# Copies of the transposed probabilities: heads innermost, half on ScalarE and half on VectorE

## The chip, the cores and the metric

One NeuronCore of a Trainium2 chip. The kernel is one launch; the metric is the device time in microseconds. Engines are named as in the profile: PE (TensorE) multiplies matrices, ACT (ScalarE) applies functions and copies, DVE (VectorE) does element-wise work and reductions, POOL (GpSimd) does element-wise work on SBUF, SP starts DMAs. PE writes into PSUM (eight banks, each 512 floats per partition here); ACT and DVE read it out.

## The reference

A small vision tower over 64 images: patches of 16 x 16 are embedded, with a class token that makes 37 tokens of 256 numbers per image. Then follow an attention with 16 heads of 16 and one shared key and value, a gated low-rank MLP, a recurrent attention, and an expert MLP with one of 8 experts per token. All is float32. The change lies in the first attention:

```python
q = (jnp.einsum('bte,oe->bto', x, Wq) + bq) * scaling
kv = jnp.einsum('bte,oe->bto', x, Wkv) + bkv
k, v = (kv[..., :HEAD_DIM], kv[..., HEAD_DIM:])
qr = q.reshape(bsz, NUM_HEADS * tgt_len, HEAD_DIM)
attn_weights = jnp.einsum('brd,bsd->brs', qr, k)
attn_probs = jax.nn.softmax(attn_weights, axis=-1)
attn_output = jnp.einsum('brs,bsd->brd', attn_probs, v)
attn_output = attn_output.reshape(bsz, NUM_HEADS, tgt_len, HEAD_DIM)
attn_output = attn_output.transpose(0, 2, 1, 3).reshape(bsz, tgt_len, EMBED_DIM)
out = jnp.einsum('bte,oe->bto', attn_output, Wo) + bo
```

The reshape of q is taken without a transpose, so the rows of an image are numbered token * 16 + head, and the output reads them in that order.

## The kernel before, in words

The kernel runs in phases with a barrier between them. The first, about the first 300 us, is embedding, attention and the logits of the gate. Images are padded to 66 and go in 22 tiles of three; two tiles are a group, so there are 11 groups, and each group has three pairs of images. The phase is a software pipeline written out by hand: a Python loop `for i in range(-1, PAIRS + 1)` on each engine issues one turn per step, in a fixed order, and the engines meet only by semaphores. In turn i PE works on the three pairs p = 3i, 3i+1, 3i+2 of group i, and puts beside them the embedding and the first transposes of group i+1 and the output projection and second transposes of group i-1. An engine takes its instructions strictly in order, so a waiting instruction holds back all that stands behind it.

What a pair of images goes through:
- `scores` (L383, PE): four products into banks 4 and 5, 16 heads x 37 keys, rows 0 to 36 for one image and 64 to 100 for the other.
- `shift_scores` (L538, L541, DVE): maximum per head, and subtraction, into the buffer `prob[p % 2]`.
- `exponentials` (L601, ACT), `sum_probs` (L549, L551, DVE), `scale_probs` (L692, POOL).
- `turn_probs` (L393, PE): eight transposes of 128 columns (two heads) each into banks 6 and 7. The even head of each two lands on partitions 0 to 36, the odd one on 64 to 100.
- `copy_probs` (L609, ACT), twice: out of PSUM into `pt`, first the even heads, then the odd ones. `pt` holds for each image 37 x 16 numbers per partition with the head innermost. Each copy walks the eight chunks outermost and the tokens innermost, so it reads PSUM contiguously and writes one float every 64 bytes.
- `mix_values` (L413, PE): 16 products of `pt` with the values, then `copy_output` (L620, ACT).

PE waits in `mix_values(p)` for both copies of p, in `turn_probs(p)` for both copies of p-1 and for `scale_probs(p)`. The copies of p wait for `mix_values(p-1)`. On PE a turn runs: scores(3i), embedding (L329), turn_probs(3i-1), embedding, mix_values(3i-1), scores(3i+1), turn_probs(3i), project(i-1) (L425), mix_values(3i), turn_first(i+1) (L340), scores(3i+2), turn_probs(3i+1), values and keys(i+1) (L371, L359), mix_values(3i+1), turn_second(i-1) (L436), queries(i+1) (L351), gate_logits(i-1) (L449). turn_first waits for `normalise_first` and turn_second for `normalise_second` (both L504, DVE); the next scores wait for `copy_queries` (L643, ACT). On POOL `spread_keys` (L683) stands between the scalings. The add of the projection on DVE is L558, its statistics L493 to L498.

Of the kernel before, what the change touches and what calls it, by code (L numbers as in the profile page):

```python
# [21 lines left out]
B, TOK, D = 64, 37, 256  # L22
# [7 lines left out]
HH = NH // 2  # L30
# [9 lines left out]
HP = 64  # L40
# [28 lines left out]
def build(nc, x_h, pack1_h, pack2_h, packc_h, w1_h, w2_h, out_h):  # L69
# [9 lines left out]
    with ExitStack() as top:  # L79
# [178 lines left out]
        with phase():  # L258
# [3 lines left out]
             v_out, k_block, scored, maxed, shifted, exped, row_sum, row_inv, scaled, p_turned, p_copied, mixed, o_copied,  # L262
# [5 lines left out]
                    "row_inv", "scaled", "p_turned", "p_copied", "mixed", "o_copied", "with_bo", "projected", "added",  # L268
# [29 lines left out]

            def probs_of(p):
                return prob[p % 2].rearrange("p (f h s) -> p f h s", f=2, h=HH)[:, :, :, 0:TOK]  # L300
# [13 lines left out]
            def _(pe):  # L314
# [72 lines left out]
                def turn_probs(p):  # L387
                    if not image_pair(p):
                        return
                    pe.wait_ge(scaled, p + 1)  # L390
                    free(pe, p_copied, 2 * p)
                    for c in range(HH):
                        mm = nc.tensor.transpose(turns_bank[:, c * 128:c * 128 + PR],  # L393
                                                 prob[p % 2][:, c * 128:(c + 1) * 128], ident[0:PR, 0:PR])
                    mm.then_inc(p_turned, 1)

                def mix_values(p):
# [4 lines left out]
                    pe.wait_ge(p_copied, 2 * (p + 1))  # L402
# [75 lines left out]
            def _(dve):  # L478
# [64 lines left out]

                def sum_probs(p):
# [27 lines left out]
                for i in range(-1, PAIRS + 1):  # L572
                    p = 3 * i
                    shift_scores(p)
                    sum_probs(p)
                    add_embedded(i + 1)
                    shift_scores(p + 1)
                    normalise_first(i + 1)
                    sum_probs(p + 1)
                    add_projected(i - 1)  # L580
                    shift_scores(p + 2)
                    normalise_second(i - 1)
# [5 lines left out]
            def _(act):  # L588
# [15 lines left out]
                def copy_probs(p, e):  # L604
                    if not image_pair(p):
# [3 lines left out]
                    nc.scalar.copy(  # L609
                        pt.rearrange("p (m t c e) -> p c m t e", m=2, t=TOK, e=2)[:, :, :, :, e],  # L610
                        turns_bank[e * HP:e * HP + TOK, :].rearrange("p (c m t) -> p c m t", c=HH, m=2)[:, :, :, 0:TOK]
                    ).then_inc(p_copied, 1)
# [33 lines left out]
                for i in range(-1, PAIRS + 1):  # L646
                    p = 3 * i
                    exponentials(p)
                    copy_probs(p - 1, 0)
                    copy_probs(p - 1, 1)  # L650
                    copy_output(p - 1)
                    copy_probs(p, 0)
                    exponentials(p + 1)
                    copy_probs(p, 1)
                    copy_output(p)
                    copy_first(i + 1)
                    copy_probs(p + 1, 0)
                    exponentials(p + 2)
                    copy_probs(p + 1, 1)
# [1241 lines left out]
```

## Time and profile before

| | us |
|---|---|
| median of 3 runs | 902.04 (899.74 to 902.21) |
| profiled execution | 892.15 |
| its span | 890.1 |
| PE busy in the span | 686.8 (77%) |
| DVE busy | 434.1 (49%) |
| ACT busy | 284.2 (32%) |
| L609, both copies of 33 pairs (66) | 76.5, 1159 ns each |

The profile comes from one execution. Its span runs from the first to the last instruction; 2.05 us of the execution's time lie around it. "Idle before" is the time for which an engine stood still ahead of an instruction, and the releaser is what the profile holds to have ended it. L609 and the like are lines of the kernel before; in the changed kernel the same instructions have other numbers. PEclk is the clock granted to PE as a share of 2.4 GHz.

### The profile page before, as it was taken

The numbers are of one execution on the slowest core, as the hardware profiler recorded it, in microseconds if no ns is written. First come the engines' busy times: TensorE is split into PE (matmuls) and PEld (weight loads), VectorE is DVE, ScalarE is ACT, GpSimd is POOL, SyncE is SP. The second block draws the span as 40 slices with busy tenths as digits, with TensorE's granted clock in tenths as the row PEclk, the third lists the DMA queues.
The fourth block names the chain that finished last, engine by engine and source line by source line (L and its number), as shares of the span: only waits on it lengthen the run. The fifth ranks groups of instructions, "written<-read, shape, count | busy, mean of one in ns | idle before, by whom it ended". The sixth has DMA issues, their size and how long they took to land. (4 is left out here: it accounts for less than half of the span.)

```text
span 890.1 us, 14154 instructions
## 1 busy us (share of the span) xinstructions
PE 686.8 (77%) x4606; PEld 521.2 (59%) x4606; DVE 434.1 (49%) x1183; ACT 284.2 (32%) x648; POOL 246.8 (28%) x330
## 2 busy tenths in 40 slices
PE   3789888888886418999996200399549999999995
PEld 2557666666663306888885100388445677666773
DVE  1355555555564282666766349366542333333331
ACT  0244454444454222434423100154302222222221
POOL 2334344344443000434343100134111222222211
PEclk9899999999999557999998555599758999999998
DMA  8111001011100000000000677332421111111110
GB/s 339 32 32 32 21 28 30 20 32 32 32 1 1 1 0 3 1 0 0 0 0 0 31 270 330 64 88 85 171 96 42 42 48 54 54 53 44 48 42 18
DMA packets 21542, 49.31 MB, mean 55 GB/s; under 512 B 12451, under 2 KB 12581, under 8 KB 20719
## 3 DMA queue, kind: packets, MB, share of 16 engines
q1 hardware_dynamic: 17583, 33.21, 12.8%
q0 software_dynamic: 3328, 10.23, 3.8%
q10 hardware_dynamic: 576, 5.15, 1.5%
q8 instruction: 33, 0.54, 0.3%
q14 instruction: 22, 0.18, 0.1%
HBM read 38.72 MB, written 9.86 MB: 55 GB/s over the span
## 5 line engine op out<-in xcount | busy, mean ns | idle before, releaser
L1793 ACT ACTIVATE work<-psum,cst 128x128 f32<-128x128 f32 x208 | 56.6, 382 | 144.1 <-PE psum L1708 144.1
L1695 PE MATMUL psum<-arena_w,work 128*128 x208 | 96.7, 609 | 1.0 <-DVE work L1747 1.0
L1719 PE MATMUL psum<-arena_w,work 128*128 x416 | 94.2, 379 | 0.4 <-ACT work L1793 0.4
L609 ACT COPY arena_w<-psum 37x592 f32<-37x592 f32 x66 | 76.5, 1159 | 54.4 <-PE psum L393 53.6
L1719 PEld LDWEIGHTS psum<-arena_w,work 128*128 128x128 f32 x416 | 77.1, 190 | 10.5 <-issue 1.1
L1352 PE MATMUL psum<-tokens,work 111*111 (+1 forms) x88 | 15.8, 305 | 73.0 <-POOL work L1320 71.8
L1756 DVE COPY work<-psum 128x512 f32<-128x512 f32 x52 | 36.0, 692 | 70.9 <-PE psum L1695 70.9
L1657 POOL DMA_INDIRECT out<-work,row_i x26 | 25.7, 987 | 161.0 <-DVE work L1769 161.0
L329 PE MATMUL psum<-arena_w 128*111 128x256 f32 x264 | 63.0, 390 | 8.7 <-DMA arena_w<-in_pack 8.7
L692 POOL TENSOR_TENSOR arena_w<-arena_w,work 101x592 f32<-101x592 f32 x33 | 39.5, 1197 | 91.5 <-DVE work L551 91.5
L1695 PEld LDWEIGHTS psum<-arena_w,work 128*128 128x128 f32 x208 | 38.6, 196 | 40.4 <-issue 40.4
L329 PEld LDWEIGHTS psum<-arena_w 128*111 128x111 f32 x264 | 45.9, 180 | 22.9 <-DMA arena_w<-in_pack 8.7
L250 POOL TENSOR_TENSOR work<-work 111x1 f32<-111x1 f32 x44 | 24.4, 555 | 118.8 <-DVE work L246 118.8
L1352 PEld LDWEIGHTS psum<-tokens,work 111*111 111x111 f32 x88 | 11.7, 188 | 74.1 <-POOL work L1320 72.1
L413 PE MATMUL psum<-arena_w 37*32 37x74 f32 x1056 | 25.5, 236 | 36.2 <-issue 25.3
L683 POOL TENSOR_TENSOR arena_w<-arena_w 128x296 f32<-128x296 f32 x66 | 43.8, 683 | 28.8 <-DVE arena_w L526 28.8
L413 PEld LDWEIGHTS psum<-arena_w 37*32 37x32 f32 x1056 | 19.8, 110 | 47.1 <-issue 33.0
L1763 DVE TENSOR_TENSOR tokens<-psum,cst 128x256 f32<-128x256 f32 x26 | 11.0, 425 | 73.5 <-PE psum L1719 73.5
L383 PE MATMUL psum<-arena_w 128*37 128x296 f32 x264 | 41.5, 436 | 3.3 <-ACT arena_w L643 3.3
L538 DVE TENSOR_REDUCE work<-psum 101x16 f32<-101x592 f32 x33 | 25.5, 773 | 34.9 <-PE psum L383 34.9
L929 PE MATMUL psum<-arena_w 128*128 128x222 f32 x176 | 40.7, 379 | 1.5 <-DVE arena_w L1069 1.0
L929 PEld LDWEIGHTS psum<-arena_w 128*128 128x128 f32 x176 | 33.9, 203 | 6.6 <-DVE arena_w L1069 2.1
(213 smaller groups left out, 1342.2 us busy)
## 6 DMA issues: line engine op xcount, KB each, us to landing
arena_w<-in_w SPq DMA_DIRECT2D x2, 4096.0 KB, 13.8
arena_w<-in_x SPq DMA_DIRECT2D x22, 333.0 KB, 2.9
x_rows<-tokens SPq DMA_DIRECT2D x22, 192.0 KB, 2.0
arena_w<-in_pack ACTq DMA_DIRECT2D x1, 2420.0 KB, 8.4
cst<-in_packc ACTq DMA_DIRECT2D x1, 1727.0 KB, 13.0
arena_w<-in_pack SPq DMA_DIRECT2D x1, 1024.0 KB, 7.5
arena_w<-in_pack ACTq DMA_DIRECT2D x1, 818.5 KB, 7.8
work<-a_rows SPq DMA_DIRECT2D x22, 32.4 KB, 2.0
```

The source lines that it names most:

```text
L329: mm = nc.tensor.matmul(bank[0][0:R, j * D:(j + 1) * D], xp[j][:, k * R:(k + 1) * R], w_lin[:, k, :], start=(k == 0), stop=(k == PC - 1))
L383: mm = nc.tensor.matmul(bank[4 + f][e * HP:e * HP + TOK, 0:HH * TOK], qt[:, a:a + TOK], kb[p % 2 * 2 + e], start=True, stop=True)
L413: mm = nc.tensor.matmul(out[32 * b:32 * (b + 1)], vpad[i % 2][:, v0:v0 + 2 * HD], probs[:, :, r0:r0 + TOK], start=(e == 0), stop=(e == 1))
L609: nc.scalar.copy(pt.rearrange("p (m t c e) -> p c m t e", m=2, t=TOK, e=2)[:, :, :, :, e], turns_bank[e * HP:e * HP + TOK, :].rearrange("p ...
L683: nc.gpsimd.tensor_tensor(kb[p % 2 * 2 + e].rearrange("p (h s) -> p h s", h=HH), kt[:, a:a + TOK].unsqueeze(1).broadcast_to([128, HH, TOK] ...
L692: nc.gpsimd.tensor_tensor(by_head(prob[p % 2], HP), by_head(prob[p % 2], HP), small[p % 2][:, 2 * NH:3 * NH].unsqueeze(2).broadcast_to([PR ...
L929: mm = nc.tensor.matmul(bank[2 + f // 2 % 2][:, (f % 2) * W:(f % 2 + 1) * W], w_out1[:, f, :], z1, start=True, stop=True)
L1352: mm = nc.tensor.matmul(bank[j][0:R, h * 128:(h + 1) * 128], ab[j][:, h * R:(h + 1) * R], tokens[0:R, bass.ds((2 * i + j) * RW + D + h * 1 ...
L1695: mm = nc.tensor.matmul(bank[2 * j + f][:, :], xgt[j][:, k * 128:(k + 1) * 128], arena_w1[:, bass.ds(expert * (2 * FF) + (k * FF + f * 512 ...
L1719: mm = nc.tensor.matmul(bank[7][:, 0:D], ht[j][:, g * 128:(g + 1) * 128], arena_w2[:, bass.ds(expert * (FC * D) + g * D, D)], start=(g == ...
L1756: nc.vector.tensor_copy(hp[j][:, f * 512:(f + 1) * 512], bank[2 * j + f][:, :]).then_inc(h_out[j], 1)
L1793: nc.scalar.activation(ht[j][:, g * 128:(g + 1) * 128], bank[4 + f][:, k * 128:(k + 1) * 128], ACT.Gelu, bias=cst[:, bass.ds(expert * FC + ...
```

## The change

The numbering of the heads in the buffer `prob` is changed: a chunk of 128 columns now holds the heads c and c+8 instead of 2c and 2c+1. After the transposes partitions 0 to 36 hold heads 0 to 7 and partitions 64 to 100 heads 8 to 15. In `pt`, whose layout is as before, each half is then eight neighbouring floats per token. The two copies of a pair walk image, token and then head: they write runs of eight floats (32 bytes) and read PSUM with a step of 128 floats (512 bytes) from one element to the next. The first half is copied by ACT, the second by DVE, each with a semaphore of its own (`p_copied`, `p_copied1`), and PE waits for both.

```diff
--- before.py
+++ after.py
@@ -259,13 +259,13 @@
...
-             v_out, k_block, scored, maxed, shifted, exped, row_sum, row_inv, scaled, p_turned, p_copied, mixed, o_copied,
+             v_out, k_block, scored, maxed, shifted, exped, row_sum, row_inv, scaled, p_turned, p_copied, p_copied1, mixed, o_copied,
-                    "row_inv", "scaled", "p_turned", "p_copied", "mixed", "o_copied", "with_bo", "projected", "added",
+                    "row_inv", "scaled", "p_turned", "p_copied", "p_copied1", "mixed", "o_copied", "with_bo", "projected", "added",
...
@@ -296,8 +296,14 @@
                 return scores_bank[0:PR, :].rearrange("p (f n) -> p f n", f=2)[:, :, 0:HH * TOK].rearrange(
                     "p f (h s) -> p f h s", h=HH)
 
+            def turns_of(e):
+                return turns_bank[e * HP:e * HP + TOK, :].rearrange("p (c m t) -> p m t c", c=HH, m=2)[:, :, 0:TOK, :]
+
+            def probs_turned(e):
+                return pt.rearrange("p (m t e c) -> p m t e c", m=2, t=TOK, e=2)[:, :, :, e, :]
+
             def probs_of(p):
-                return prob[p % 2].rearrange("p (f h s) -> p f h s", f=2, h=HH)[:, :, :, 0:TOK]
+                return prob[p % 2].rearrange("p (h f s) -> p f h s", f=2, h=HH)[:, :, :, 0:TOK]
 
             @block.sync
             def _(sp):
@@ -388,7 +394,8 @@
                     if not image_pair(p):
                         return
                     pe.wait_ge(scaled, p + 1)
-                    free(pe, p_copied, 2 * p)
+                    free(pe, p_copied, p)
+                    free(pe, p_copied1, p)
                     for c in range(HH):
                         mm = nc.tensor.transpose(turns_bank[:, c * 128:c * 128 + PR],
                                                  prob[p % 2][:, c * 128:(c + 1) * 128], ident[0:PR, 0:PR])
@@ -399,7 +406,8 @@
                         return
                     i = p // 3
                     pe.wait_ge(v_out, i + 1)
-                    pe.wait_ge(p_copied, 2 * (p + 1))
+                    pe.wait_ge(p_copied, p + 1)
+                    pe.wait_ge(p_copied1, p + 1)
                     if p % 3 == 0:
                         pe.wait_ge(q_out, 2 * (i + 1))
                     free(pe, o_copied, p)
@@ -541,6 +549,13 @@
                     nc.vector.tensor_tensor(probs_of(p), scores_of(), mx.unsqueeze(3).broadcast_to([PR, 2, HH, TOK]),
                                             ALU.subtract).then_inc(shifted, 1)
 
+                def copy_probs(p):
+                    if not image_pair(p):
+                        return
+                    dve.wait_ge(p_turned, p + 1)
+                    free(dve, mixed, p)
+                    nc.vector.tensor_copy(probs_turned(1), turns_of(1)).then_inc(p_copied1, 1)
+
                 def sum_probs(p):
                     if not image_pair(p):
                         return
@@ -573,12 +588,15 @@
                     p = 3 * i
                     shift_scores(p)
                     sum_probs(p)
+                    copy_probs(p - 1)
                     add_embedded(i + 1)
                     shift_scores(p + 1)
+                    copy_probs(p)
                     normalise_first(i + 1)
                     sum_probs(p + 1)
                     add_projected(i - 1)
                     shift_scores(p + 2)
+                    copy_probs(p + 1)
                     normalise_second(i - 1)
                     keys_and_values(i + 1)
                     sum_probs(p + 2)
@@ -601,15 +619,12 @@
                     nc.scalar.activation(by_head(prob[p % 2], HP), by_head(prob[p % 2], HP), ACT.Exp,
                                          scale=HD ** -0.5).then_inc(exped, 1)
 
-                def copy_probs(p, e):
+                def copy_probs(p):
                     if not image_pair(p):
                         return
                     act.wait_ge(p_turned, p + 1)
                     free(act, mixed, p)
-                    nc.scalar.copy(
-                        pt.rearrange("p (m t c e) -> p c m t e", m=2, t=TOK, e=2)[:, :, :, :, e],
-                        turns_bank[e * HP:e * HP + TOK, :].rearrange("p (c m t) -> p c m t", c=HH, m=2)[:, :, :, 0:TOK]
-                    ).then_inc(p_copied, 1)
+                    nc.scalar.copy(probs_turned(0), turns_of(0)).then_inc(p_copied, 1)
 
                 def copy_output(p):
                     if not image_pair(p):
@@ -646,17 +661,14 @@
                 for i in range(-1, PAIRS + 1):
                     p = 3 * i
                     exponentials(p)
-                    copy_probs(p - 1, 0)
-                    copy_probs(p - 1, 1)
+                    copy_probs(p - 1)
                     copy_output(p - 1)
-                    copy_probs(p, 0)
+                    copy_probs(p)
                     exponentials(p + 1)
-                    copy_probs(p, 1)
                     copy_output(p)
                     copy_first(i + 1)
-                    copy_probs(p + 1, 0)
+                    copy_probs(p + 1)
                     exponentials(p + 2)
-                    copy_probs(p + 1, 1)
                     copy_output(p + 1)
                     copy_second(i - 1)
                     copy_queries(i + 1)
```

The order on DVE, in the part of a turn from the shift of pair 3i+1 to that of pair 3i+2. Before (L538, L541 shift; L504 normalise; L549, L551 sum; L558 to L498 add the projection):

```order
L538 TENSOR_REDUCE work<-psum 101x16
L541 TENSOR_TENSOR arena_w<-psum,work 101x16x37
L504 TENSOR_SCALAR work<-tokens,work 111x256 x2
L549 TENSOR_REDUCE work<-arena_w 101x16
L551 RECIPROCAL work<-work 101x16
L558 TENSOR_TENSOR tokens<-psum,tokens 111x2x256
L493 BN_STATS work<-tokens 111x6 x2
L496 BN_AGGR work<-work 111x2 x2
L498 TENSOR_SCALAR work<-work 111x2
L538 TENSOR_REDUCE work<-psum 101x16
L541 TENSOR_TENSOR arena_w<-psum,work 101x16x37
```

After, the same part (now L546, L549 shift; L512 normalise; L564, L566 sum; L573 to L506 add the projection; L557 the copy):

```order
L546 TENSOR_REDUCE work<-psum 101x16
L549 TENSOR_TENSOR arena_w<-psum,work 101x2x8x37
L557 COPY arena_w<-psum 37x74x8
L512 TENSOR_SCALAR work<-tokens,work 111x256 x2
L564 TENSOR_REDUCE work<-arena_w 101x16
L566 RECIPROCAL work<-work 101x16
L573 TENSOR_TENSOR tokens<-psum,tokens 111x2x256
L501 BN_STATS work<-tokens 111x6 x2
L504 BN_AGGR work<-work 111x2 x2
L506 TENSOR_SCALAR work<-work 111x2
L546 TENSOR_REDUCE work<-psum 101x16
L549 TENSOR_TENSOR arena_w<-psum,work 101x2x8x37
```

A copy of 37 x 74 x 8 stands between the shift and the normalisation behind it; another stands behind the second shift, ahead of the second normalisation. A third stands ahead of L521, behind the sum of the turn's first pair.

The order on ACT, from the exponentials of pair 3i on. Before (L601 exponentials, L609 copy, L620 output of the mixing, L628 first transposes):

```order
L601 ACTIVATE arena_w<-arena_w 101x16x37
L609 COPY arena_w<-psum 37x8x74 x2
L620 COPY arena_w<-psum 128x2x74
L609 COPY arena_w<-psum 37x8x74
L601 ACTIVATE arena_w<-arena_w 101x16x37
L609 COPY arena_w<-psum 37x8x74
L620 COPY arena_w<-psum 128x2x74
L628 COPY work<-psum 128x444
```

After (L619 exponentials, L627 copy, L635 output, L643 first transposes):

```order
L619 ACTIVATE arena_w<-arena_w 101x16x37
L627 COPY arena_w<-psum 37x74x8
L635 COPY arena_w<-psum 128x2x74
L627 COPY arena_w<-psum 37x74x8
L619 ACTIVATE arena_w<-arena_w 101x16x37
L635 COPY arena_w<-psum 128x2x74
L643 COPY work<-psum 128x444
```

The second copy of each pair is gone: the output of the mixing follows at once behind the first copy of pair 3i-1, and behind the exponentials of the pair after.

## Rows read from the trace of the kernel before

**Rows 1.** Two turns: us, busy PE, PEld, DVE, ACT, POOL; clock, DMA share.

```profile
102.36:125.28 22.92, 20.39 (x228) 15.12 (x229) 13.44 (x32) 11.40 (x16) 10.09 (x12) 1.00 0.12 31
125.28:149.70 24.42, 21.91 (x230) 16.53 (x230) 13.45 (x32) 11.38 (x16) 10.09 (x12) 0.93 0.11 30
```

**Rows 2.** Timeline of one turn: start us, us, engine, line, [idle before <-releaser].

```profile
112.07 1.91 PE L425 MATMUL psum<-arena_w 128*111 128x256 f32 x8
...
112.27 1.18 ACT L609 COPY arena_w<-psum 37x592 f32<-37x592 f32 x1 [1.65 <-PE psum L393]
...
112.34 0.77 DVE L541 TENSOR_TENSOR arena_w<-psum,work 101x592 f32<-101x592 f32 x1
...
112.37 1.32 POOL L683 TENSOR_TENSOR arena_w<-arena_w 128x296 f32<-128x296 f32 x2
...
113.03 1.14 DVE L504 TENSOR_SCALAR work<-tokens,work 111x256 f32<-111x256 f32 x2
...
113.99 1.14 ACT L609 COPY arena_w<-psum 37x592 f32<-37x592 f32 x1
...
115.21 1.20 POOL L692 TENSOR_TENSOR arena_w<-arena_w,work 101x592 f32<-101x592 f32 x1 [1.52 <-DVE work L551]
...
115.23 0.72 PE L413 MATMUL psum<-arena_w 37*32 37x74 f32 x32 [1.25 <-issue]
...
116.72 0.17 DVE L498 TENSOR_SCALAR work<-work 111x2 f32<-111x2 f32 x1
...
117.53 0.91 PE L393 MATMUL psum<-cst,arena_w 101*128 101x101 f32 x8
...
117.65 0.78 DVE L538 TENSOR_REDUCE work<-psum 101x16 f32<-101x592 f32 x1 [0.76 <-PE psum L383]
...
119.15 0.73 DVE L504 TENSOR_SCALAR work<-tokens,work 111x256 f32<-111x256 f32 x2
...
120.20 1.16 ACT L609 COPY arena_w<-psum 37x592 f32<-37x592 f32 x1
...
121.46 0.72 PE L413 MATMUL psum<-arena_w 37*32 37x74 f32 x32 [1.10 <-DVE arena_w L528]
...
124.44 0.78 ACT L643 ACTIVATE arena_w<-psum,arena_w 128x222 f32<-128x222 f32 x2 [1.17 <-PE psum L351]
...
125.28 1.20 PE L383 MATMUL psum<-arena_w 128*37 128x296 f32 x8 [0.17 <-ACT arena_w L643]
```

**Rows 3.** The same columns, three stretches around the second mixing.

```profile
118.00:121.40 3.40, 2.36 (x34) 1.86 (x31) 2.85 (x7) 2.85 (x3) 1.37 (x2) 1.00 0.00 0
213.50:216.90 3.40, 2.31 (x55) 1.86 (x53) 2.62 (x7) 2.53 (x3) 1.36 (x3) 1.00 0.00 0
216.90:220.30 3.40, 3.40 (x12) 3.17 (x13) 0.00 (x0) 0.81 (x2) 2.50 (x4) 0.50 0.00 0
```

**Rows 4.** Groups by form: copies out of PSUM; busy us, mean ns.

```profile
L609 ACT COPY arena_w<-psum 37x592 f32<-37x592 f32 x66 | 76.5, 1159 | 54.4 <-PE psum L393 53.6
...
L634 ACT COPY arena_w<-psum 128x444 f32<-128x444 f32 x11 | 5.8, 529 | 12.9 <-PE psum L436 12.9
...
L1066 DVE COPY arena_w<-psum 128x222 f32<-128x222 f32 x11 | 4.2, 383 | 4.1 <-PE psum L915 4.1
...
L1756 DVE COPY work<-psum 128x512 f32<-128x512 f32 x52 | 36.0, 692 | 70.9 <-PE psum L1695 70.9
```

**Rows 5.** The instructions of line 1570: duration ns min/median/max.

```profile
L1570 DVE COPY work<-psum x1: 342/342/342, 642.5 to 642.5; 111x176 f32<-111x176 f32 x1
```

**Rows 6.** Timeline, copy of the queries: first and last turn.

```profile
29.08 0.78 ACT L643 ACTIVATE arena_w<-psum,arena_w 128x222 f32<-128x222 f32 x2 [6.53 <-PE psum L351]
...
267.90 0.78 ACT L643 ACTIVATE arena_w<-psum,arena_w 128x222 f32<-128x222 f32 x2 [1.17 <-PE psum L351]
```

**Rows 7.** Timeline, mixing in the last turns, first and last of four.

```profile
274.61 0.99 PE L413 MATMUL psum<-arena_w 37*32 37x74 f32 x32 [3.83 <-issue]
...
294.97 1.21 PE L413 MATMUL psum<-arena_w 37*32 37x74 f32 x32 [2.44 <-issue]
```


## The prediction

> **What bounds the kernel now.** I read the page first for where the time lies, then the windows of the turns, then the timeline of one turn. The change touches only the attention phase, about 20 to 297 us of the 890.1 us span. Its steady part is ten turns from one copy of queries to the next: the first starts at 29.08, the last of the eleven at 267.90, so ten turns take 238.8 us, 23.88 each [rows 6]. There are two sorts of turn: 22.92 us with the granted clock at 1.00, TensorE busy for 20.39 of it, and 24.42 us at 0.93, busy for 21.91 [rows 1]. TensorE is the bound. It waits three times in a turn; the reader should look for where, in the turn that ends at 125.28 [rows 2]:
> - before the mixing of pair 3i (115.23) TensorE stood 1.25 us. Its last work ended at 112.07+1.91 = 113.98; ACT's second copy ran 113.99 to 115.13, behind the first (112.27, 1.18) and behind the exponentials that are issued between them. The bracket says "issue", but the end of the copy and the start agree to 0.1 us.
> - before the mixing of pair 3i+1 (121.46) it stood 1.10 us. The bracket names L528 on DVE, whose product that mixing doesn't need; ACT's second copy ends at 120.20+1.16 = 121.36, and that is what it waited for.
> - before the scores of the next turn (125.28) it stood 0.17 us for the copied queries (124.44). The change leaves this.
> The mixing of pair 3i-1 comes behind two embeddings, which hide its copies: nothing to gain there in a full turn.
> So the two copies in a row on ACT end last at two of three mixings, for 2.35 us a turn.
>
> **What the new copies cost.** L609 takes 1159 ns for 592 elements on ACT. The other ACT copy out of PSUM takes 529 for 444, which is some 650 for 592 if I take 160 of it as fixed [rows 4]. The old copy writes each element 64 bytes from the one before, and pays 1.78 times for it. The new one writes eight side by side and steps 512 bytes in PSUM between reads. ACT: between 650 and 2 x 1159 = 2320 ns; I keep 1159, the row of the same tile. It decides little: between the end of the transposes and the moment when DVE is done with its half, ACT has 1.68 us for pair 3i (112.27 to 113.95, worked out below).
> DVE: its copies out of PSUM take 383 for 222 and 692 for 512, 1.066 ns per element, so 777 for 592 [rows 4]. L1570, a count per tile and expert that is turned to expert and tile on its way out, reads PSUM at a stride of eight floats and takes 342 for 176 elements; the line through the two others gives 334 [rows 5]. So a stride alone costs DVE nothing there. I take 0.78 us, the low end. The high end is ACT's strided price paid on the read and on the write, 2.32 us; both ends stay in the range. Below 0.78 I see no reason.
> The Trainium skill, "Advanced Engine Details and Errata", section "Memory Cachelines", says that SBUF has lines of 16 bytes and wants two hits in one before the access is at full speed. By that rule the new writes are at full price, and L609's 1.78 fits it. The same section gives PSUM lines of 8 bytes, of which the new reads use half; that would make the copy dearer, and is a rival below. L1570 also takes one element per such line, and shows no price.
>
> **The turn after, step by step** (times of rows 2, the turn's start at 125.28-22.92 = 102.36). Up to the transposes of pair 3i nothing moves: DVE's new copy of pair 3i-1 falls into its wait for the second embedding.
> 1. Pair 3i. ACT copies 112.27 to 113.45. DVE's half stands behind the shift of pair 3i+1, which ends at 112.34+0.77 = 113.11; it runs 113.13 to 113.91. TensorE is free at 113.98, so mixing starts there: 1.25 earlier.
> 2. Behind that copy on DVE stand the first normalisation, the sum of pair 3i+1, the adding of the projection and the next shift. The normalisation took 1.14 beside POOL's L683 (112.37, 1.32), and 0.73 at 119.15 where POOL is free of such work; it now starts at 113.93, behind L683, so I take 0.73 and it ends at 114.66, 0.49 later than before (114.17). TensorE wants it at 113.98+0.65: no wait worth a term.
> 3. Sum and reciprocal took 1.04 from there to POOL's scaling (115.21); scaling now runs 115.70 to 116.90 (1.20). With an estimated 0.15 for the handovers the transposes of pair 3i+1 start at 117.05. TensorE could have started at 113.98+(117.53-115.23) = 116.28, so 0.77 us of the gain turns into **a new wait**. Net gain here: 117.53-117.05 = 0.48.
> 4. From those transposes TensorE works 120.36-117.53 = 2.83 us to the next mixing: ready at 119.88. DVE: the adding and statistics ended at 116.89, now 0.49 later at 117.38, shift (two of 0.78, 1.59 with handovers) to 119.09, copy of pair 3i+1 to 119.88. ACT's, from 118.0, ends at 119.2. Mixing starts at 119.93 against 121.46: 1.53 earlier. Both DVE and TensorE arrive together, so DVE is now level with TensorE in this half of the turn.
> 5. The second normalisation is behind that copy: 119.90 to 120.63, and the transposes that need it could start at 119.93+0.65 = 120.58: 0.1 lost. The rest takes 125.28-121.46 = 3.82, so the next scores start at 123.85. The turn is 21.49 instead of 22.92: **1.43 less, ten times, 14.3 us**.
> TensorE's additional semaphores lie on instructions that wait anyway: nothing.
> 6. The last turns have nothing that hides the copies: four mixings, the first at 274.61 and the last at 294.97 [rows 7], stand behind both ACT copies. The last three win one ACT copy each, some 1.24 us as in step 1. The first wins 0.4, since DVE's half comes behind the sum of the next pair there. That makes 4.1 us.
>
> **The clock.** The ten turns exceed 10 x 22.92 by 9.6 us, some six and a half dips of 1.5 us. The granted clock is 0.50 (1.2 GHz) in 216.9:220.3, right behind a stretch in which TensorE was busy for 2.31 of 3.40 us, with the 1.10 us wait in it; a like stretch with 2.36 of 3.40 left the clock at 1.00, 2.4 GHz [rows 3]. The two are so near that taking most of the wait out should take some dips with it. But the new wait of 0.77 comes close ahead of it. From zero to all 9.6 us can go; I take three of the six and a half, 4.5 us.
>
> **Sum.** 14.3 + 4.1 + 4.5 = 22.9 us off the profiled execution, 892.15 (span 890.1 and 2.05 around it), gives 869. The median of the runs is 902.04, 9.9 us above the profiled one for a reason the trace can't show; I take the same 22.9 off it, 879, and round to **880**.
>
> **Rivals.**
> - *The dips stay as often as they are.* For it: the products of values, keys and mixing, which stand around the wait in the stretch before a dip, stay as they are. Against: the two stretches above are so near to each other. Then 902.04-18.4 = 884.
> - *A PSUM read at 512 bytes costs DVE what the 64-byte write cost ACT.* Factor 1.78 on 777 ns: 1.38 us. Two copies a turn are on DVE's chain, so 1.20 of the 1.43 goes: 2.3 us in ten turns, 2.1 in the last, dips as now: 898. For it: L609. Against: L1570, though at a smaller step and in one bank. This is also where the Trainium skill's lines of PSUM ("Advanced Engine Details and Errata", "Memory Cachelines") would lead if they hold for DVE.
> - *Slower: DVE becomes the bound.* From a copy of 0.78+1.43/2 = 1.50 us on, each turn is longer than before, since both copies delay the normalisation, the sum, POOL's scaling and the transposes behind it. At the upper end, 2.32 us, a turn grows by 2 x 1.54-1.43 = 1.65, ten times 16.5, the end by 0.5: 919. For it: nothing in the trace copies across two PSUM banks at such steps. Against: the same rows 5.
> - That the change doesn't do what it says: the ACT copy might stay at 1159 for its reads. It costs nothing by step 1, so it is no case of its own.
>
> **How the numbers follow.** Forecast 0.50 (880), dips stay 0.29 (884), dear PSUM reads 0.14 (898), slower 0.07 (919). The first two are faster; of the third I count 0.08 as faster, 0.05 as within 0.3% (2.7 us, what a measurement of this kernel can tell from no change), 0.01 as slower. So faster 0.87, same 0.05, slower 0.08. Range: all dips gone and the sum right gives 874, with 2 us for what moves in later phases 872; up to the third case, 897.
>
> **What would show it.** Right: DVE's copy near 0.78 us; TensorE's waits before two mixings near zero; a new wait of 0.7 to 0.8 before the transposes of pair 3i+1, released by POOL; turns of 21.5 us at clock 1.00 and fewer at a lower one. Wrong: a DVE copy above 1.2 us (then the third or fourth case), turns at 1.00 still near 22.9, or more dips than seven.

## The result, and the profile after

| | before | after |
|---|---|---|
| median, us | 902.02 (899.74 to 902.21, 4) | 864.55 (863.81 to 865.10, 4) |
| profiled execution | 892.15 | 865.10 |
| its span | 890.1 | 863.3 |
| ten turns of the attention phase | 238.82 | 214.97 |
| turn at full clock | 22.92 | 21.48 |
| last copy of queries to last gate logits | 39.37 | 36.96 |
| copy on ACT / DVE, ns | 1159 / - | 765 / 777 |

The ratio of the changed kernel to the one before is 0.960 [0.957, 0.963]. Repeated on another chip, with six executions against eleven, it is 0.963 [0.958, 0.969]. Forecast were 880 us and a range of 872 to 897: the change gained 37.5 us where 22.9 were counted. Executions of the kernel before scatter over some 20 us (889 to 912 over all that were timed), those of the changed kernel over some 6, and the ratios here and below leave out executions more than 1.5% above the fastest of their kernel, so that they are nearer to 1 than a quotient of the medians. This scatter turned out to be part of the answer.

First the windows, in the columns of [rows 1] but cut from one copy of the queries to the next: the ten turns, then two neighbouring ones (us; busy us of PE, PEld, DVE, ACT and POOL; granted clock; DMA share and GB/s).

```profile
29.36:244.33 214.97, 201.23 (x2215) 147.54 (x2216) 150.59 (x329) 69.57 (x127) 99.42 (x119) 0.99 0.11 30
136.94:158.42 21.48, 20.48 (x230) 15.13 (x230) 15.41 (x34) 7.13 (x13) 10.10 (x13) 1.00 0.12 33
158.42:179.89 21.47, 20.47 (x230) 15.13 (x230) 15.41 (x34) 7.13 (x13) 10.08 (x13) 1.00 0.12 33
```

The clock is 0.99 over all ten turns, and 1.00 in each after the first. The turns are alike to 0.02 us. PE is busy for 20.48 of 21.48 us, against 20.39 of 22.92 in [rows 1].

A turn as in [rows 2]; it starts at 116.30. L549 is the second half of the shift, L627 and L557 are the copies on ACT and DVE, L512 the normalisation, L704 POOL's scaling, L400 the transposes of the probabilities, L421 the mixing.

```profile
116.30 1.20 PE L389 MATMUL psum<-arena_w 128*37 128x296 f32 x8 [0.17 <-ACT arena_w L658]
...
126.03 1.91 PE L433 MATMUL psum<-arena_w 128*111 128x256 f32 x8
...
126.28 0.78 DVE L549 TENSOR_TENSOR arena_w<-psum,work 101x592 f32<-101x592 f32 x1
...
126.23 0.77 ACT L627 COPY arena_w<-psum 37x592 f32<-37x592 f32 x1 [1.66 <-PE psum L400]
...
127.09 0.78 DVE L557 COPY arena_w<-psum 37x592 f32<-37x592 f32 x1
...
127.79 0.72 DVE L512 TENSOR_SCALAR work<-tokens,work 111x256 f32<-111x256 f32 x2
...
128.08 0.72 PE L421 MATMUL psum<-arena_w 37*32 37x74 f32 x32
...
129.55 1.20 POOL L704 TENSOR_TENSOR arena_w<-arena_w,work 101x592 f32<-101x592 f32 x1 [1.91 <-DVE work L566]
...
130.81 0.91 PE L400 MATMUL psum<-cst,arena_w 101*128 101x101 f32 x8 [0.35 <-POOL arena_w L704]
...
131.76 0.77 ACT L627 COPY arena_w<-psum 37x592 f32<-37x592 f32 x1 [1.87 <-PE psum L400]
...
132.92 0.78 DVE L557 COPY arena_w<-psum 37x592 f32<-37x592 f32 x1
...
133.62 0.72 DVE L512 TENSOR_SCALAR work<-tokens,work 111x256 f32<-111x256 f32 x2
...
133.96 0.72 PE L421 MATMUL psum<-arena_w 37*32 37x74 f32 x32 [0.33 <-DVE arena_w L557]
```

The bracketed waits of 1.25 and 1.10 us before the mixing are down to nothing (128.08) and 0.33 (133.96), and a new one of 0.35 stands before the transposes of pair 3i+1 (130.81), released by POOL. The two copies by form, as in [rows 4]:

```profile
L557 DVE COPY arena_w<-psum 37x592 f32<-37x592 f32 x33 | 25.6, 777 | 2.3 <-PE psum L400 1.2
...
L627 ACT COPY arena_w<-psum 37x592 f32<-37x592 f32 x33 | 25.2, 765 | 57.7 <-PE psum L400 57.7
```

And the four mixings of the last turns, of which [rows 7] has the first and the last, with the transposes and the projection behind the first:

```profile
250.89 1.40 PE L421 MATMUL psum<-arena_w 37*32 37x74 f32 x32 [3.68 <-DVE arena_w L557]
...
254.34 1.61 PE L400 MATMUL psum<-cst,arena_w 101*128 101x101 f32 x8
255.75 2.60 PE L433 MATMUL psum<-arena_w 128*111 128x256 f32 x8
258.27 0.72 PE L421 MATMUL psum<-arena_w 37*32 37x74 f32 x32
...
262.91 0.72 PE L421 MATMUL psum<-arena_w 37*32 37x74 f32 x32 [1.95 <-DVE arena_w L557]
...
269.01 1.21 PE L421 MATMUL psum<-arena_w 37*32 37x74 f32 x32 [1.07 <-DVE arena_w L557]
```

The same stretch in the kernel before, the second and third mixing included:

```profile
277.65 1.21 PE L393 MATMUL psum<-cst,arena_w 101*128 101x101 f32 x8
...
278.70 1.91 PE L425 MATMUL psum<-arena_w 128*111 128x256 f32 x8
...
281.85 0.72 PE L413 MATMUL psum<-arena_w 37*32 37x74 f32 x32 [1.24 <-issue]
...
287.50 0.72 PE L413 MATMUL psum<-arena_w 37*32 37x74 f32 x32 [2.97 <-issue]
```

The four waits add up to 6.70 us (3.68, 0, 1.95, 1.07) where they were 10.48 (3.83, 1.24, 2.97, 2.44). They are no longer for ACT's second copy: the bracket names DVE's. But part of this gain is lost again, since TensorE runs longer at half clock here: over the 20 us from the last copy of the queries on, the granted clock is 0.82 against 0.91, and the first mixing, the transposes and the projection behind it take 1.5 us more (1.40, 1.61 and 2.60 against 0.99, 1.21 and 1.91).

### The profile page after: what moved, and what is told of

It reads as the page before. It is cut to its first block and busy times, and to the rows that moved or that the text cites. A ratio compares the mean times of both kernels' runs of the same rounds, so it can differ in the third digit from the quotient of the medians.

```text
span 863.3 us, 14177 instructions
## 1 busy us (share of the span) xinstructions
PE 678.2 (79%) x4606; PEld 513.0 (59%) x4606; DVE 455.9 (53%) x1216; ACT 237.3 (27%) x615; POOL 246.7 (29%) x330
## 5 line engine op out<-in xcount | busy, mean ns | idle before, releaser
L704 POOL TENSOR_TENSOR arena_w<-arena_w,work 101x592 f32<-101x592 f32 x33 | 39.5, 1197 | 71.8 <-DVE work L566 71.8
L941 PE MATMUL psum<-arena_w 128*128 128x222 f32 x176 | 39.8, 372 | 1.7 <-DVE arena_w L1081 1.0
L627 ACT COPY arena_w<-psum 37x592 f32<-37x592 f32 x33 | 25.2, 765 | 57.7 <-PE psum L400 57.7
L546 DVE TENSOR_REDUCE work<-psum 101x16 f32<-101x592 f32 x33 | 25.4, 771 | 24.2 <-PE psum L389 24.2
L253 DVE TENSOR_SCALAR work<-tokens,work 111x256 f32 (+1 forms) x44 | 22.5, 512 | 29.5 <-POOL work L250 29.5
L955 PE MATMUL psum<-arena_w 128*128 128x222 f32 x176 | 36.2, 357 | 0.0
```

The source lines that it names most:

```text
L704: nc.gpsimd.tensor_tensor(by_head(prob[p % 2], HP), by_head(prob[p % 2], HP), small[p % 2][:, 2 * NH:3 * NH].unsqueeze(2).broadcast_to([PR ...
L941: mm = nc.tensor.matmul(bank[2 + f // 2 % 2][:, (f % 2) * W:(f % 2 + 1) * W], w_out1[:, f, :], z1, start=True, stop=True)
L955: mm = nc.tensor.matmul(bank[1][:, W:2 * W], w_in2[:, f, :], hid[:, f * W:(f + 1) * W], start=(f == 0), stop=(f == OC - 1))
```

## The experiments

Medians are of all timed executions of a run; "before" is timed anew beside each group.

**The kernel before, once more.** No edit.

> The kernel before, unchanged, to see its executions once more. Four timed executions took 902.0 us (median), the profiled one 892.15, the changed kernel 864.55. Theory A (dips of the clock): the 9.9 us between are more dips of the granted clock in executions that fall differently against it; so this one's mean clock is lower than 0.867 where its time is near 902, and the ten turns of the attention phase take more than 238.8 us. Theory B: the 9.9 us lie in other phases or in waits that have nothing to do with the clock; then the ten turns take 238.8 us whatever the time of the execution.

Measured: 893.97 us (890.26 to 909.06, 11 executions), and the kernel before beside it 899.68 (889.31 to 909.04, 13); ratio 0.9985 [0.994, 1.003]. The profile caught one of 909.06. Its ten turns and one of its stretches at low clock (same columns):

```profile
29.40:287.51 258.11, 230.60 (x2215) 169.52 (x2216) 131.78 (x300) 110.83 (x156) 100.98 (x121) 0.86 0.09 25
130.40:140.60 10.20, 9.88 (x64) 7.50 (x65) 2.27 (x5) 1.81 (x5) 3.57 (x5) 0.52 0.00 0
```

Ten turns take 258.11 us, 19.3 more than the 238.82 of the first profile, at a mean clock of 0.86 against 0.95; the whole span is 17.0 us longer (907.1 against 890.1). So all of the difference lies in these turns. Its PE rows show where:

```profile
130.72 1.15 PE L413 MATMUL psum<-arena_w 37*32 37x74 f32 x32 [1.09 <-DVE arena_w L528]
...
132.60 3.20 PE L351 MATMUL psum<-work,arena_w 128*128 128x222 f32 x8
...
139.18 3.77 PE L329 MATMUL psum<-arena_w 128*111 128x256 f32 x12
```

The dip starts behind the same wait of 1.09 us ahead of the mixing of pair 3i+1, but lasts 10.2 us instead of 3.4, and takes in the queries (3.20 us for what takes 1.74 at full clock) and part of the next embedding. Such turns take 27.4 us. Over the 24 timed executions of both copies of this kernel the mean clock falls as the span grows: 0.870 at 887.6, 0.867 at 892.0, 0.860 at 897.7, 0.854 at 903.7, 0.849 at 907.1. An estimate from two of these: 0.133 of 892.0 is 118.6 us of clock that was not granted, 0.146 of 903.7 is 131.9, so 13.3 us more for a span that is 11.7 longer. Theory A holds. The wait does not bring a dip each time: the last turn here and three of ten in the first profile have it too (1.09 to 1.10 us) and take 22.9.

**New walk, no split.** The kernel before with the numbering and the walk of the changed one (`probs_turned` and `turns_of` as there); both copies stay on ACT, in their old places around the exponentials. The edit against the kernel before, cut:

```diff
-                return prob[p % 2].rearrange("p (f h s) -> p f h s", f=2, h=HH)[:, :, :, 0:TOK]
+                return prob[p % 2].rearrange("p (h f s) -> p f h s", f=2, h=HH)[:, :, :, 0:TOK]
...
-                    nc.scalar.copy(
...
+                    nc.scalar.copy(probs_turned(e), turns_of(e)).then_inc(p_copied, 1)
```

> The new numbering of the heads and the new walk, but both copies of a pair on ACT in the order of the kernel before. Theory A (the price of one copy decides): a copy costs 0.77 us on ACT as in the changed kernel, so the mixing of pair 3i waits 0.7 us instead of 1.25, that of pair 3i+1 0.4 instead of 1.10; a turn takes 21.7 us at full clock, 0.2 more than with the split, and the dips of the clock go: about 867 us. Theory B (the split decides): a turn takes 22.3 us or more, since two copies in a row still stand before each mixing, and the dips stay: 885 us or more.

Measured: 872.68 us (869.45 to 874.24); ratio to before 0.970 [0.961, 0.978]; turns of 21.86 at full clock.

```profile
L615 ACT COPY arena_w<-psum 37x592 f32<-37x592 f32 x66 | 50.6, 766 | 56.2 <-PE psum L399 55.4
```

```profile
114.33 0.72 PE L419 MATMUL psum<-arena_w 37*32 37x74 f32 x32 [0.77 <-issue]
...
119.97 0.72 PE L419 MATMUL psum<-arena_w 37*32 37x74 f32 x32 [0.51 <-issue]
```

766 ns a copy, and waits of 0.77 and 0.51 before the two mixings. Both numbers are near theory A, the turn 0.16 longer than worked out. In the profiled execution the clock is at half for some 17 us across the first two turns, which take 25.34 and 24.32; these 5.9 us over two full turns are as much as lies between the median and the 867 expected.

**Split, no new walk.** The changed kernel with the old numbering and the old walk, reading and writing, on both engines (cut; `...` in a line stands for left-out arguments):

```diff
-                return pt.rearrange("p (m t e c) -> p m t e c", ...)[:, :, :, e, :]
+                return pt.rearrange("p (m t c e) -> p c m t e", ...)[:, :, :, :, e]
```

> The split over ACT and DVE with the old numbering and the old walk (one float every 64 bytes). If DVE pays nothing for the scattered write, its copy takes 0.78 us, ACT's 1.16 is hidden, and the kernel takes what the changed one does, 865 us, turns of 21.5. If DVE pays the factor that ACT pays (1.78, or 1159 against 650), its copy takes 1.38 us, two of them on its chain make the turn 1.2 us longer, 22.7, and the time 877 to 892, the latter if the dips come back.

Measured: 873.78 us (872.27 to 876.85); ratio 0.973 [0.964, 0.981]; turns of 22.17, no dip after the first. The two copies, then the mixings of pairs 3i and 3i+1 in one turn:

```profile
L557 DVE COPY arena_w<-psum 37x592 f32<-37x592 f32 x33 | 38.7, 1172 | 2.3 <-PE psum L400 1.2
...
L627 ACT COPY arena_w<-psum 37x592 f32<-37x592 f32 x33 | 38.6, 1171 | 57.0 <-PE psum L400 57.0
```

```profile
109.11 0.72 PE L421 MATMUL psum<-arena_w 37*32 37x74 f32 x32 [0.54 <-issue]
...
115.29 0.72 PE L421 MATMUL psum<-arena_w 37*32 37x74 f32 x32 [0.71 <-DVE arena_w L557]
```

DVE pays for the scattered write too: 1172 ns, 1.5 times its 777, the factor of ACT's 1159 to 765. Neither branch of the expectation had that value, and the median lies below the 877 to 892 of the second. Each 0.395 us of copy lengthened the turn by 0.69, 1.75 times as much, against the factor of 2 in the prediction's working. Walk alone and split alone gain nearly the same, and both together 864.55: the two parts overlap, since each of them alone already shortens both waits and takes the dips out of the full turns. A wait of 0.71 us ahead of pair 3i+1 brings none in nine turns.

**Keys twice.** The kernel before, with a second, redundant pass over the keys:

```diff
-                    for k in range(2):
+                    for k in (0, 1, 0, 1):
                         mm = nc.tensor.matmul(bank[3][:, 0:G], w_k[:, k, :], ...
```

> The kernel before, with the four key products of each group computed twice over (same result, 1.02 us of TensorE work more per turn), in the place where TensorE would wait 1.10 us for the copies of pair 3i+1. Theory A (the wait brings the dips): the work fills the wait, the dips go, all turns take about 22.9 us: ten turns 229 instead of 238.8, and the kernel, doing more work, is faster than before, by 10 us in a profile of 238.8 and by up to 20 against 902. Theory B (the dips come from something else): no change in the dips, the time is that of before or up to 1 us a turn longer, 902 to 912.

Measured: 885.76 us (883.35 to 891.76); ratio 0.988 [0.978, 0.997].

```profile
30.19:264.15 233.96, 212.74 (x2255) 158.44 (x2256) 131.83 (x300) 110.99 (x157) 100.17 (x120) 0.97 0.10 28
```

```profile
116.08 0.72 PE L413 MATMUL psum<-arena_w 37*32 37x74 f32 x32 [1.25 <-issue]
...
120.19 1.77 PE L359 MATMUL psum<-work,arena_w 128*128 128x222 f32 x8
...
122.29 0.72 PE L413 MATMUL psum<-arena_w 37*32 37x74 f32 x32 [0.33 <-issue]
```

The keys take 1.77 us instead of 1.02, the wait behind them is 0.33 instead of 1.10, and a turn at full clock is 22.92 as before. TensorE does more work and the kernel is faster. In the ten turns the clock is 0.97 and one dip is left beside the first turn's, which is long (26.34 us), so that the ten take 233.96 and not the 229 expected. Of the 8.7 us between the spans of the two profiled executions 4.9 lie in the ten turns; the other 3.8 lie outside them, behind the attention phase for the most part, and stay open. Theory A holds, in that the filled wait leaves one dip in nine turns; it doesn't take out every one.

**DVE's copy twice.** The changed kernel, plus a copy into a buffer that nobody reads:

```diff
+                    nc.vector.tensor_copy(spare.rearrange(...), turns_of(1)).then_inc(spared, 1)
                     nc.vector.tensor_copy(probs_turned(1), turns_of(1)).then_inc(p_copied1, 1)
```

> The changed kernel, with DVE copying its half twice, the first time into a spare buffer that nobody reads; nothing else differs. One DVE copy becomes some 1.58 us. Step by step as in the prediction both of a turn's later copies lie on DVE's chain: a turn at full clock takes 21.48 + 2 x 0.80 = 23.1, or 22.9 with the slope of the split-only run (0.69 for 0.39 on each of two). Theory A (TensorE's waits bring the dips): the waits are as long as before the change, so dips come back and executions scatter as those of before: 880 to 905. Theory B (it was the walk or the split itself that took the dips away): full-clock turns throughout, 864.6 + 15 + 2 = 882, with little scatter. Rival of the chain: DVE has slack for one of the two copies, and the turn takes 22.3.

Measured: 890.68 us (883.03 to 903.82, 10 executions) beside 905.52 (889.45 to 909.23, 13) of before; ratio 0.994 [0.988, 1.000].

```profile
28.95:268.75 239.80, 213.07 (x2215) 157.50 (x2216) 170.55 (x358) 69.58 (x128) 99.57 (x119) 0.94 0.10 27
```

```profile
164.75 0.72 PE L423 MATMUL psum<-arena_w 37*32 37x74 f32 x32 [0.84 <-issue]
...
167.49 0.91 PE L402 MATMUL psum<-cst,arena_w 101*128 101x101 f32 x8 [0.36 <-POOL arena_w L708]
...
171.35 0.72 PE L423 MATMUL psum<-arena_w 37*32 37x74 f32 x32 [1.04 <-DVE arena_w L561]
```

Full-clock turns of 22.85, which is the 22.9 with the measured slope. The waits are 0.84, 0.36 and 1.04, and the dips are back: turns of 24.3 among those of 22.9, 239.8 us for ten, a clock of 0.94, and a scatter of 21 us. Neither the walk nor the split as such keeps the dips away; the length of the waits decides. Theory A again. It also says what a DVE copy of 1.55 us would have cost: 1.37 of the 1.44 us that a full turn gains, and the dips.

**Both copies on ACT, back to back.** The new-walk kernel with one line moved per pair:

```diff
                     copy_probs(p, 0)
-                    exponentials(p + 1)
                     copy_probs(p, 1)
+                    exponentials(p + 1)
```

> New numbering and walk, both copies on ACT as in the layout-only run, but one right behind the other ahead of the next exponentials, nothing on DVE. Two copies of 0.77 end at 112.27 + 1.53 = 113.80 on the clock of the turn of before, while TensorE is busy to 113.98; the exponentials are 0.7 us later, the first normalisation and the sum need no copy ahead of them. Theory A (only the price of a copy and DVE's chain count): a turn of 21.2 to 21.4, that is 862 to 864 us, at least as good as the split. Theory B (two copies in a row on one engine always cost a wait): 21.9 as in the layout-only run, 869 to 874.

> Both copies on ACT, back to back, once more beside the changed kernel. If the 0.40 us per turn (21.08 against 21.48) and the shorter last turns hold, it is 4 to 7 us faster than the changed kernel, a ratio of 0.992 to 0.995; if the difference before was one of chips, the two are within 2 us.

Measured: 858.22 us (857.01 to 863.12), ratio to before 0.956 [0.947, 0.966]; again, beside the changed kernel, 859.63 (858.25 to 863.61), ratio to before 0.955 [0.950, 0.960]. Turns of 21.08 and 21.09.

```profile
152.24 0.91 PE L399 MATMUL psum<-cst,arena_w 101*128 101x101 f32 x8 [0.54 <-POOL arena_w L695]
...
153.19 1.56 ACT L615 COPY arena_w<-psum 37x592 f32<-37x592 f32 x2 [2.05 <-PE psum L399]
...
155.00 0.72 PE L419 MATMUL psum<-arena_w 37*32 37x74 f32 x32
...
168.75 1.56 ACT L615 COPY arena_w<-psum 37x592 f32<-37x592 f32 x2 [1.65 <-PE psum L399]
...
170.41 0.72 PE L419 MATMUL psum<-arena_w 37*32 37x74 f32 x32
```

Two copies in a row take 1.56 us (153.19 and 168.75), and neither mixing waits (155.00, 170.41); what is left is 0.54 before the transposes (152.24). Without a copy on DVE ahead of them, normalisation and sum are in time. Theory A holds, and the second engine is not needed. The turn is 0.1 us shorter than the 21.2 to 21.4 expected; the two profiled executions, 863.12 and 863.61, are the longest of theirs, and both medians lie below the 862 to 864 expected.

**Reordered.** The changed kernel, with three things moved:

```diff
+                    values(i + 1)
                     turn_probs(p + 1)
-                    values(i + 1)
                     keys(i + 1)
```

and on DVE the shift of pair 3i+2 behind the keys, on ACT its exponentials behind the copy of the queries.

> The changed kernel with the waits that it left attacked: on TensorE the values of the next group are computed ahead of the transposes of pair 3i+1 (they fill the wait for POOL's scaling, 0.36 us in the profile); on DVE the copy of pair 3i+1, the second normalisation and the keys come ahead of the shift of pair 3i+2; on ACT the exponentials of pair 3i+2 come last in the turn. If the waits of 0.36 and 0.33 and the handovers behind them go, a turn takes 20.6 to 20.9 instead of 21.48: 856 to 859 us. Rival: the shift that is moved back delays the next turn's first pair, since the next scores wait for it, and the turn stays at 21.5 or grows.

Measured: 861.51 us (859.80 to 862.91); ratio to before 0.961 [0.951, 0.971]; turns of 20.72. A full turn is 0.76 us shorter, as expected, but the median is only 3 below the changed kernel's and misses the 856 to 859. In the profiles the ten turns take 208.27 us, 6.7 less. From the last copy of the queries on, the profile is 2.2 us longer (858.8-237.6 = 621.2 against 863.3-244.3 = 619.0), at a granted clock of 0.64 over the first 90 of them against 0.68. That leaves the 4.5 us between the profiled executions; this one lies 0.9 under its median, that of the changed kernel 0.55 above its own, which makes 3.

**Mixed split.** Reordered, with only pair 3i+1 split (DVE's copies of the two other pairs are gone, which the cut doesn't show):

```diff
+                    if p % 3 != 1:
+                        nc.scalar.copy(probs_turned(1), turns_of(1)).then_inc(p_copied1, 1)
```

> The reordered kernel, but only pair 3i+1 is split over ACT and DVE; of the pairs 3i-1 and 3i ACT copies both halves back to back, so that DVE's chain ahead of the scaling is one copy shorter. In the back-to-back run the scaling of pair 3i+1 ended 2.89 us after the mixing of pair 3i began (149.3, 152.19); with the values of the next group in between TensorE asks for it after 3.26 us, so the wait of 0.54 is gone, and the mixing of pair 3i+1 starts when the keys are done, 0.6 us earlier. A turn of 20.5 us, ten of them 6 us less than in the back-to-back run: 852 to 855 us. Rival: the bound is the shift of pair 3i+2, which the next scores wait for, and the turn stays at the 20.72 of the reordered run: 857 to 860.

Measured: 859.88 us (857.58 to 863.44); ratio to before 0.956 [0.951, 0.961]; turns of 20.63, 0.13 more than worked out; the median misses the 852 to 855 expected.

```profile
164.06 0.72 PE L421 MATMUL psum<-arena_w 37*32 37x74 f32 x32
...
167.20 0.91 PE L400 MATMUL psum<-cst,arena_w 101*128 101x101 f32 x8
...
169.18 0.72 PE L421 MATMUL psum<-arena_w 37*32 37x74 f32 x32 [0.29 <-DVE arena_w L557]
```

The wait before the transposes is gone (167.20), one of 0.29 before the mixing stays. The ten turns take 205.1 us against 212.5 of the back-to-back kernel, and yet the medians are level. In the two profiles the last turns (38.9 against 36.8) and the phases behind (584.1 against 582.0) take back 4.3 of it, with a granted clock of 0.64 against 0.70 over the first 90 us behind the last copy of the queries. The profiled execution is still 4.7 us the faster one (858.88 against 863.61), but it lies 1.0 under its median, and the other 4.0 above. The time is in the rival's 857 to 860, though not by the turn of 20.72 that the rival named.

**The changed kernel again.**

> The changed kernel once more, on the chip of the other two, to tell whether they beat it. Theory A (the changed kernel has no dips in its full turns in any execution): 863 to 866 us in all executions, where the kernel before scatters over some 20 us. Theory B (it was luck of one chip): executions up to 15 us longer are among them.

Measured: 866.85 us (864.13 to 870.22, 6 executions) beside 903.39 (892.46 to 912.29, 11). Turns of 21.48 again, but the first takes 23.17 instead of 21.67: the half-clock stretch ahead of it lasts 13.7 us instead of 6.8 and reaches into it, and one of 3.4 follows in both profiles. Neither theory named that: behind the first turn nothing varies, but the start can differ, and the executions lie 6 us apart, up to 870.22 where theory A said 866. The back-to-back kernel on the same chip is faster than it: 858.25 to 863.61 against 864.13 to 870.22, ratio of the means 0.992, and 0.989 to 0.995 by the spread of the six and six.

**Projection twice.** The kernel before, with half of the projection done again:

```diff
-                    for j in range(2):
+                    for j in (0, 1, 1):
```

> The kernel before, with half of the output projection computed twice (same result, 0.95 us of TensorE work), right ahead of the mixing of pair 3i, where TensorE waits 1.25 us. The wait ahead of pair 3i+1 (1.10 us) stays. The keys-twice run filled that second wait and left one dip in nine full turns. Theory A1 (the second wait, between values, keys and mixing, brings the dips): here the dips stay, the mean clock is as low as before, turns of 22.9 and 24.4 to 27.4 alternate, 890 to 905 us. Theory A2 (either wait counts): the dips get rare here too, and the time falls to 883 to 890.

Measured: 903.37 us (897.63 to 909.64) beside 904.77 (895.05 to 909.45, 7); ratio 1.003 [0.994, 1.013].

```profile
28.98:276.70 247.72, 227.34 (x2251) 168.42 (x2252) 131.80 (x300) 111.09 (x157) 101.34 (x121) 0.90 0.09 26
```

```profile
123.95 0.72 PE L413 MATMUL psum<-arena_w 37*32 37x74 f32 x32 [0.39 <-issue]
...
130.17 0.72 PE L413 MATMUL psum<-arena_w 37*32 37x74 f32 x32 [1.09 <-DVE arena_w L528]
```

The wait ahead of pair 3i is filled from 1.25 to 0.39 (123.95), the one ahead of pair 3i+1 is as long as before (130.17). The dips stay, ten turns take 247.7 us at a clock of 0.90. Theory A1: it is the wait ahead of pair 3i+1 that brings them. Together with the others: at 1.01 to 1.10 us of it there are dips, while at 0.71 (split alone), 0.51 (walk alone) and 0.33 (changed kernel) none starts behind the first turn, and one in nine turns at 0.33 with the keys computed twice. Where between 0.71 and 1.01 they begin was not tried.

## Why the prediction was wrong, step by step

- *What bounds the kernel, and steps 1 to 5*: right. The turn was forecast at 21.49 us and takes 21.48. Counted from the turn's start, the mixing of pair 3i was put at 11.62 (measured 128.08-116.30 = 11.78), the transposes of pair 3i+1 at 14.69 (14.51), the mixing of pair 3i+1 at 17.57 (17.66). The 14.3 us are 14.4. Two slips change nothing: step 4 has the shift of pair 3i+2 end at 119.09, where 117.38 and 1.59 make 118.97, and the 113.95 for the end of DVE's first copy is the 113.91 of step 1.
- *The new wait* was forecast at 0.77 us, released by POOL. It is there, with 0.35: TensorE is ready 0.2 later than worked out, the scaling ends 0.1 earlier, and the handover takes 0.06 instead of 0.15. Against that the mixing of pair 3i+1 starts 0.26 behind the end of DVE's copy (132.92+0.78 = 133.70, 133.96), where 0.05 stood. That these errors cancel to 0.01 us a turn is luck.
- *Price of a copy*: DVE's 0.78 is 0.777; the stride in PSUM costs nothing. ACT's 1.16 is 0.77. As said, this decided nothing in the split kernel: ACT's copies end at 127.00 and 132.53, and 0.39 more would still be ahead of the mixings at 128.08 and 133.96. But it hid a better one: with 0.77 both copies fit on ACT, and had I worked that case out I should have seen it. Where the prediction says of the lines of SBUF that the new writes are "at full price", full speed is meant.
- *Step 6, the last turns*: 4.1 us forecast, 2.4 measured. The waits shrink by 3.8 (0.15, 1.24, 1.02 and 1.37 where 0.4 and three times 1.24 stood), so the step is nearly right. What it leaves out is the clock again: the longer stretch at half clock takes some 1.5 us back.
- *The clock*: here the prediction failed. I took three of six and a half dips, 4.5 us; in the profiles 9.6 us of dips became 0.2, so 9.4. That leaves 14.4+9.4+2.4 = 26.2 of the 27.05 us between the profiled executions, and 0.8 elsewhere, most of it in the later phases.
- *"For a reason the trace can't show; I take the same 22.9 off it"*: the second half of the failure, 10.4 us. The reason was the same term. The repeat profile of the kernel before shows that longer executions are longer by dips in these very turns, 19.3 us at the far end. Shortening the wait takes out all dips of the median execution, some 9.4+10.4 = 20 us where 4.5 stood, if what lies between the profiled executions and the medians is dips as well. The lower end of the range was built from the profile's 9.6 alone, and so it ended at 872.
- *Rivals*: the dips stayed away, so the first fell. The dear PSUM read fell with 777 ns. With it fell, for a read by DVE, the use that the prediction made of the lines of PSUM in the Trainium skill ("Advanced Engine Details and Errata", section "Memory Cachelines"): the trace shows no price for steps of 512 bytes. The slower case fell for the same reason, but the twice-copied run shows that its mechanism is sound: at 1.55 us of copy the turn is back at 22.85. The turning point of 1.50 us was a little low: at 1.55 the turn is still 0.07 us short of 22.92, and the slope of the split-only run puts it at 1.60.

That the wait ahead of pair 3i+1 brings the dips is shown, by filling it (keys twice), by restoring it (DVE's copy twice) and by filling most of the other one without effect (projection twice). That the 902.02 of the first comparison was made of dips is shown at both ends, at 892.15 (9.6 us over ten full turns) and at 909.06 (28.9), once between in the kernel with the projection twice (898.95, 18.3), and by the mean clock of the timed executions; an execution of the kernel before at 902 itself was not profiled. Why the same wait is followed by a dip in some turns and by none in others, and why a dip lasts 3.4 us in some executions and 10.2 in others, stays open.

## What to carry to other kernels

When a trace shows stretches at half clock behind a wait of the TensorE, price the wait twice: its own length, and all the dips behind it. And when the profiled execution is faster than the median, look for the term that can vary between executions before taking the difference as fixed; here it was the very term that the change removed. Before work is split over two engines, work out what the cheaper form of it does on the one that has it: the walk alone, well placed, beat walk and split together by 0.8% and was level with the best split that was tried (859.63 against 859.88 us).

## What was not expected of the hardware

- A copy of 37 x 592 floats that reads PSUM at 512-byte steps takes 777 ns on DVE, just what the line through its contiguous copies gives, and 765 on ACT, 0.1 us above the estimate from [rows 4]. A write of one float every 64 bytes costs 1159 to 1172 ns on either engine. The Trainium skill, "Advanced Engine Details and Errata", section "Memory Cachelines", names lines of 16 bytes in SBUF; both engines agree with it in that writes of 32 bytes at a time have no such price.
- A wait of 1.1 us in every 22.9 us, where it was followed by stretches at half clock, made the kernel's time scatter by 2%. With 0.33 in its place the full turns of the changed kernel did not vary by more than 0.02 us.
- Filling that wait with redundant products made the kernel 1.2% faster [0.3% to 2.2%].
